# Four attention blocks on one core: which engine issues the transfers of the softmax shifts

## The reference

```python
# block 0: group norm (16 groups), 8 heads of 16 channels
xn = _group_norm(x, scale, bias); q, k, v = split(xn @ w_qkv)
scores = jax.nn.softmax(einsum('bcq,bck->bqk', q, k) * hd ** (-0.5), axis=-1)
x = einsum('bqk,bck->bqc', scores, v) @ w_out + b_out + x
# block 1: group norm (32 groups), 8 heads, biases; the skip adds the normed input
# block 2: layer norm, one head of 128 channels; block 3: group norm (32), one head of 128
```

## Time and profile before

| | |
|---|---|
| median of three runs | 2102.32 us (2099.62 to 2107.74) |
| the profiled execution | 2101.81 us, its span 2100.0 us |
| PE matmul, PE weight load busy | 2042.0 us, 1151.2 us |
| VectorE, ScalarE, GpSimd busy | 1679.7, 1490.2, 407.7 us |
| mean granted TensorE clock | 0.984 |
| queue q1 | 48400 packets, 94.81 MB |

### The profile page before, as it was taken

The page is one execution under the profiler, slowest core; times in us unless marked ns, Lnnn a source line. Parts: engine busy times, 40 slices in busy tenths (PEclk is TensorE's granted clock), DMA queues, the critical chain, the costliest instruction groups (busy, mean ns, idle before and its releaser), DMA issues.

```text
span 2100.0 us, 40993 instructions
## 1 busy us (share of the span) xinstructions
PE 2042.0 (97%) x15879; PEld 1151.2 (55%) x15879; DVE 1679.7 (80%) x3104; ACT 1490.2 (71%) x2722; POOL 407.7 (19%) x541
## 2 busy tenths in 40 slices
PE   4899999999999999999999999999999989999999
PEld 3444444444744467443774448644585436847988
DVE  6899999999799877898779886899868967773433
ACT  1487787888588855988469875698647976497555
POOL 3102111220122311122120221203111040021231
PEclk7799999999999999999999999999999999999999
DMA  5322351432132314031230502304040050000000
GB/s 148 70 34 63 51 102 42 72 72 32 53 60 56 47 32 81 12 80 23 56 67 2 102 2 64 59 2 102 2 106 7 2 102 2 7 7 2 11 1 21
DMA packets 48592, 97.42 MB, mean 46 GB/s; under 512 B 7824, under 2 KB 10640, under 8 KB 48272
## 3 DMA queue, kind: packets, MB, share of 16 engines
q1 hardware_dynamic: 48400, 94.81, 21.4%
HBM read 55.98 MB, written 37.75 MB: 45 GB/s over the span
## 4 chain that ended last, share of the span: by engine, by line
PE 82%; DVE 11%; DMA 2%; issue 1%; ACT 1%; SPq 1%; POOL 0%; POOLq 0%; DVEq 0%; ACTq 0%
PE outs L1451 19%; PE banks L1413 14%; PE banks L1426 12%; PE outs L1491 12%; DVE part_max L1204 9%; PE banks L1469 9%; PE banks L1332 7%; PE banks L1338 5%; PE banks L1341 5%; DMA q_stack<-shift_parts 2%; ACT probs L1093 1%; SPq L888 1%; DVE stats L1142 0%; PE banks L1399 0%; DVE o_turn L1216 0%
## 5 line engine op out<-in xcount | busy, mean ns | idle before, releaser
L1204 DVE TENSOR_REDUCE part_max<-banks 128x1 f32<-128x512 f32 x2048 | 1273.9, 680 | 179.2 <-PE banks L1413 173.9
L1093 ACT ACTIVATE probs<-banks 128x512 f32<-128x512 f32 x2048 | 1059.9, 609 | 192.6 <-PE banks L1426 166.2
L1413 PE MATMUL banks<-k_stack,q_stack 62*128 62x512 f32 x2048 | 564.0, 447 | 3.4 <-DVE part_max L1204 1.1
L1451 PE MATMUL outs<-probs,v_heads 128*32 128x512 f32 (+1 forms) x5136 | 561.1, 518 | 0.5
L1426 PE MATMUL banks<-q_stack,k_stack 64*128 64x512 f32 x2048 | 518.5, 444 | 19.5 <-DMA q_stack<-shift_parts 18.6
L1413 PEld LDWEIGHTS banks<-k_stack,q_stack 62*128 62x128 f32 x2048 | 262.3, 187 | 287.4 <-DVE part_max L1204 116.8
L1426 PEld LDWEIGHTS banks<-q_stack,k_stack 64*128 64x128 f32 x2048 | 242.9, 186 | 226.7 <-DVE part_max L1204 71.5
L1100 ACT ACTIVATE probs<-banks,neg_max 128x1024 f32<-128x1024 f32 x128 | 142.8, 1116 | 235.1 <-DVE neg_max L1236 194.2
L1491 PEld LDWEIGHTS outs<-v_full,probs 128*128 128x128 f32 x2048 | 257.7, 191 | 49.9 <-issue 41.3
L1491 PE MATMUL outs<-v_full,probs 128*128 128x128 f32 x2048 | 279.1, 279 | 0.1
L1236 DVE TENSOR_REDUCE neg_max<-banks 128x1 f32<-128x1024 f32 x128 | 156.5, 1223 | 138.6 <-PE banks L1469 137.9
(11 more groups left out here) (110 smaller groups left out, 1131.7 us busy)
## 6 DMA issues: line engine op xcount, KB each, us to landing
k_scratch<-parts SPq DMA_DIRECT2D x64, 256.0 KB
q_scratch<-parts SPq DMA_DIRECT2D x64, 256.0 KB
k_stack<-k_scratch SPq DMA_DIRECT2D x64, 256.0 KB, 6.9
q_stack<-q_scratch SPq DMA_DIRECT2D x64, 256.0 KB, 9.6
k_stack<-k_scratch SPq DMA_DIRECT2D x64, 128.0 KB, 8.2
q_stack<-q_scratch SPq DMA_DIRECT2D x64, 128.0 KB, 10.7
q_stack<-shift_parts SPq DMA_DIRECT2D x256, 4.0 KB
tmp<-x SPq DMA_DIRECT2D x7, 512.0 KB, 3.4
```

Source lines behind the costliest of these rows:

```text
L1093: nc.scalar.activation(probs[:, plan.prob[u], 2 * n + half, :], banks[:, plan.banks["pair", t][k], :], ACT.Exp, scale=HEAD_SCALE).then_inc ...
L1204: nc.vector.tensor_reduce(part_max[:, r % 2, column:column + 1], bank_of(("tile", r, n)), AX_X, ALU.max, negate=True).then_inc(tile_max, 1)
L1413: nc.tensor.matmul(bank_of(("tile", r, n)), qs[rows, i, a, heads, P * t:P * (t + 1)], ks[rows, i, keys, heads, :], start=True, stop=True). ...
L1451: last = nc.tensor.matmul(outs[2 * HD * n:2 * HD * (n + 1), columns], v_heads[:, i, key, at:at + 2 * HD], probs[:, plan.prob[u], n, column ...
```

## The change

`shift(r)` is taken from SyncE's walk through the list and put, word for word but for the engine, into GpSimd's. The wait for VectorE's subtraction and the four transfers of each round are now GpSimd's; they go through GpSimd's own queue. Sizes, targets, semaphores and their counts are the same, and PE waits for them at the same place.

```diff
@@ block.sync
-                def shift(r):
-                    first, a, i = heads_of(r)
-                    sp.wait_ge(*taken("shift", r))
-                    for half in range(2):
-                        for j in range(SHIFT):
-                            at = ROWS * (half + 1) - SHIFT + j
-                            row = qs[at:at + 1, i, a, first:first + GROUP // 2, :]
-                            part = shift_parts[TILES // 4 * half:TILES // 4 * (half + 1), j, :]
-                            sp.dma_start(row.rearrange("o h (n q) -> o (h n) q", n=QT).bitcast(F32),
-                                         part.bitcast(F32)).then_inc(shift_in[r % 2], 16)
@@
-                    elif kind == "shift":
-                        shift(item[1])
@@ block.gpsimd
+                def shift(r):
+                    first, a, i = heads_of(r)
+                    pool.wait_ge(*taken("shift", r))
+                    for half in range(2):
+                        for j in range(SHIFT):
+                            at = ROWS * (half + 1) - SHIFT + j
+                            row = qs[at:at + 1, i, a, first:first + GROUP // 2, :]
+                            part = shift_parts[TILES // 4 * half:TILES // 4 * (half + 1), j, :]
+                            nc.gpsimd.dma_start(row.rearrange("o h (n q) -> o (h n) q", n=QT).bitcast(F32),
+                                         part.bitcast(F32)).then_inc(shift_in[r % 2], 16)
@@
                     if kind == "outputs":
                         scale_outputs(item[1])
+                    elif kind == "shift":
+                        shift(item[1])
```

## The result

The changed kernel is slower: median 2140.22 us (2138.06 to 2144.2, four runs) against 2105.03 us, a ratio of 1.0168 with a 95% interval of 1.013 to 1.0207. The profiled execution took 2138.06 us with a span of 2136.3 us, 36.3 us longer than before. Forecast were 2101 us and a range of 2089 to 2130; the measured time lies above it.

What follows compares the result with a forecast made beforehand. VectorE's row maxima pace the first quarter, TensorE's own queue mostly the rest. Terms: 9.3 (tight rounds) + 3 (GpSimd's queue) - 14.3 (loaded rounds) = -2 us, giving about 2100, rounded up to 2101 us; 8-in-10 range 2089 to 2130.

Steps and rivals of the forecast that it cites:

- the part on what is removed: SyncE loses 256 issues and 64 waits; its scratch writes and reads move up by at most 2.7 us, worth nothing.
- loaded rounds: Six rounds whose shift transfers lie in q1 behind stack refill reads, landing 4.73 to 11.57 us after the last issue.
- The price in the tight rounds: TensorE waits longer for shifts landing 1.75 us later at 1.1 us an issue: 9.3 us lost, round 0 included.
- 18 tight rounds: Rounds beside round 0 whose shifts land under 1.75 us before TensorE needs them, mean slack 1.04 us; 14 among the first 20.
- The sentence on the Trainium skill's figures: GpSimd's slower first byte alone would land shifts 0.4 us later at equal issue cost, the sum near 8 us lower.
- The price on GpSimd's queue: Work queued behind the shift on GpSimd waits: 0.6 us at each of five phase ends, 3 us; splits and norms nothing.
- The gain in the loaded rounds: On their own queue shifts land 7 us after first issue despite refill reads: 14.3 us gained, mostly in round 59.
- The refill still blocks: Rival, slower: small packets still wait behind refill packets, the 14.3 us stay away, 2114 to 2128 us; chance 0.14.
- GpSimd's issue is dearer: Rival, slower: at 1.28 us an issue or more, first pairs of rounds come later, +13 us, 2115 us; chance 0.22.
- Cheap issue and full relief: Rival, faster: an issue of 0.9 us or less and relief of about 16 us give -12 us, 2090 us; chance 0.17.
- The chance of 0.36 for slower: Chance of slower by more than 0.5%: 0.22 for a dearer GpSimd issue plus 0.14 for a refill that still blocks.
- rounding up: The forecast of about 2100 us was raised to 2101, since an unseen wait behind GpSimd can only add.

Runs made afterwards that it cites:

- gate at five rounds: Changed kernel, with SyncE waiting for the landing of the shift transfers in rounds 1, 6, 9, 13 and 17 alone: 2101.73 us, ratio 0.9986.
- the held reads: Kernel before, with stack reads q1 and k1 held until the next shift, GpSimd issuing shifts and SyncE waiting for their landing: 2087.8 us, ratio 0.9935.

## Why the prediction was wrong

**The step that failed** is the first half of the part on what is removed: "Its writes and reads to the scratch move up by at most the 2.7 us of four issues; PE has no wait on a stack read, so this is worth nothing." I asked who waits for a read that comes earlier, and not what an earlier read runs into. SyncE loses not just the four issues but its wait for the subtraction as well (1013.0 us in all, which I had read as a sign that SyncE bounds nothing), and the order of the two kinds of transfer turns round in five rounds. Five waits of 5.2 to 7.3 us, 29 us more than before, are the price. The other 7 of the 36 us go with the clock: TensorE is busy 10 us longer in this stretch at the same work (432.74 against 422.71 us), and the granted clock falls to its half level in these stalls, each time after TensorE has stood idle. Two of the five windows:

```profile
218.00:228.00 10.00, 6.11 (x44) 2.65 (x48) 3.70 (x7) 3.92 (x8) 0.06 (x1) 0.66 1.03 167
...
495.00:506.00 11.00, 6.18 (x40) 2.49 (x44) 3.61 (x7) 3.91 (x8) 0.67 (x2) 0.53 1.06 149
```

All I needed was in the list of items: in five places the shift stands right before four reads. One of them, round 6, I had even counted among the loaded rounds, as one whose reads lie ahead of the shift; they lie behind it, and the sixth round of that kind is 50.

**The price in the tight rounds** was mis-sized, term by term. I took 1.1 us for an issue; it is 0.54 us. From the subtraction to the landing a quiet round takes 3.5 us, not 5.6, and is 0.3 us faster than before, not 1.75 slower. Of the 18 tight rounds only the three that the reads now run into (1, 13 and 17) and round 63 (below) make TensorE wait. So the 9.3 us for the tight rounds are nothing, and they don't turn into a gain either (gate at five rounds: 0.9986 with 1 in its interval), as slack ends no wait. The sentence on the Trainium skill's figures (DMA: Bandwidth & Descriptors, section Specifications: about 1 us to the first byte on GpSimd's path and 0.6 us on SyncE's) gave the wrong sign here. In quiet rounds the first 512-byte packet starts 1.14 us after the start of the first issue on GpSimd and 1.27 us on SyncE, and the last transfer lands 1.1 us after the end of the last issue on both.

**The price on GpSimd's queue** (3 us) came out near the 2.4 us that round 63 waits, but by luck: I had priced work queued behind the shift, and no such wait of TensorE for a split or a norm step appears. Round 63's shift itself starts late.

**The gain in the loaded rounds** (14.3 us) mostly didn't come. Round 59 lands 11.4 us after the subtraction instead of 12.7, where I had 7; round 42 became later. Round 18 did become quick (3.5 us), but because the reads before it had started 5 us earlier and the stall of round 17 had put it off by 10 us; with the gate at five rounds it lands at 8.1 us as before. The rounds 19 to 59 gained 2 us together.

**The rivals.** "The refill still blocks" was the right mechanism in the wrong rounds: I priced it as a gain that stays away in the six loaded rounds and never asked if quiet rounds could become loaded. "GpSimd's issue is dearer" fell. Of "Cheap issue and full relief" the cheap issue came true and the relief did not. The chance of 0.36 for slower was for reasons of which one is half true.

## What to carry to other kernels

An in-order queue that issues transfers is also a gate: an item on it that waits holds back everything behind it. Before a transfer is moved to another queue, list what stands behind it and ask what those transfers meet when they start without it; if it is something urgent and small, keep a wait where the item was. And where a small urgent transfer waits for large ones, moving half of the large ones behind it can help more than a second queue; here it gave 0.8%.

## What the runs showed of the hardware

**Four transfers of 4 KB against 3 MB.** Quiet: 3.5 us (GpSimd) or 3.8 us (SyncE, ScalarE) from subtraction to landing. The reads on another queue, ahead by 0.3 to 2.4 us: 8 to 13 us, hardware or software queue alike. The reads ahead on the same queue: 23 to 27 us where all were issued just before the shift (6.5 to 8.7 of it until the shift's first issue), 7.5 to 13.7 us where the last of them was issued 3 to 9 us before the subtraction (the six loaded rounds before the change). The Trainium skill's page DMA: Bandwidth & Descriptors, section Issuing engines are not separate DMA queues, says that a further issuing engine only saves the time of issuing; the runs add that it also removes an order, and that between the two queues 4 KB can lose some 5 to 9 us.

**GpSimd starts 3.3 us late, twice.** In rounds 32 and 63 of every kernel in which GpSimd issues, the first transfer starts 3.3 us after the subtraction instead of 0.3, though GpSimd is idle, as the changed kernel shows in round 63 (1923.10 to 1926.39). In rounds 16, 25, 26 and 33 it starts 1.3 us after the subtraction because GpSimd is still at work, a queueing that I had allowed for only in rounding up.

```profile
1922.82 0.28 DVE L1196 TENSOR_TENSOR shift_parts<-banks,shift_parts 16x128 fp32r<-16x128 f32 x1 [2.25 <-ACT shift_parts L1071]
...
1926.39 2.17 POOL L1002 DMA_DIRECT2D q_stack<-shift_parts  x4 [7.56 <-issue]
```

In the expectation for the held reads I blamed a bias addition ahead of the shift; the trace shows none. In round 63 VectorE is idle as well in this time. What holds GpSimd isn't in the profile and stays open.

**A stall costs more than its length.** In all five rounds the granted clock is 0.53 to 0.66 of full speed over the 10 or 11 us around the stall, so part of the work behind it runs at the 1.2 GHz level. 29 us of added waits became 36 us.
